# A graph-network kernel: another order of its beginning, gathers one tile ahead, and a step that gathers a whole block

## The reference, cut to what matters

```python
xs, xd = x[edge_src], x[edge_dst]                     # 53125 x 32 each
sh1 = sqrt(3) * edge_vec / norm(edge_vec)
w  = mlp(emb, fc1_w1, fc1_w2)                          # 10 -> 16 -> 512 per edge
s_t, v_t = bilinear(xs, xd, sh1, w)
w2 = mlp(emb, fc2_w1, fc2_w2)                          # 10 -> 16 -> 384 per edge
scal, gates, vecs = bilinear2(s_t, v_t, sh1, w2)
edge_out = concat(tanh(scal), vecs * tanh(gates)) * norm
return layernorm(x + segment_sum(edge_out, edge_dst))  # 3125 x 32
```

## Time and profile before

| | us |
|---|---|
| runs of the kernel before | 744.56, 744.84, 747.78 (median 744.84) |
| the profiled execution | 744.64 |
| its span, first to last instruction | 742.8 |
| PE busy / DVE busy / ACT busy / POOL busy | 687.2 / 691.7 / 560.2 / 528.0 |
| mean granted PE clock | 0.97 |
| first instruction of the first products (L751) | 37.64 |

### The profile page before, as it was taken

How to read it: one execution, slowest core, us unless ns; L and a number is a source line. 1 busy time by engine, 2 the same in 40 slices (tenths; PEclk the granted TensorE clock), 3 DMA queues, 4 the chain that set the end, 5 groups by cost and what they waited for, 6 DMA issues and landing times.

```text
span 742.8 us, 19328 instructions
## 1 busy us (share of the span) xinstructions
PE 687.2 (93%) x5990; PEld 282.9 (38%) x5990; DVE 691.7 (93%) x1231; ACT 560.2 (75%) x1281; POOL 528.0 (71%) x653
## 2 busy tenths in 40 slices
PE   2359999999999999999999999999999999999984
PEld 2113334434443444344344444334434443444321
DVE  7488999999999999999999999999999999999986
ACT  3238887887888778888888888877788888878752
POOL 5676888778876887688768886787778876887200
PEclk7569999999999999999999999999999999999998
DMA  5412211111111211121112111211121111111000
GB/s 132 112 34 47 47 32 28 40 46 28 30 42 27 50 26 42 28 47 31 43 26 45 29 43 27 48 31 27 40 46 29 28 39 26 41 27 27 20 1 23
DMA packets 45822, 28.49 MB, mean 38 GB/s; under 512 B 23299, under 2 KB 43941, under 8 KB 45721
## 3 DMA queue, kind: packets, MB, share of 16 engines
q1 hardware_dynamic: 31402, 19.43, 9.9%
q0 software_dynamic: 13312, 6.84, 6.0%
q10 hardware_dynamic: 1006, 0.96, 0.5%
HBM read 22.46 MB, written 4.74 MB: 37 GB/s over the span
## 4 chain that ended last, share of the span: by engine, by line
PE 87%; DVE 4%; issue 2%; ACT 1%; POOL 1%; DVEq 0%; ACTq 0%
PE ps L1073 16%; PE ps L986 14%; PE ps L1004 13%; PE ps L993 9%; PE ps L1053 8%; PE ps L974 6%; PE ps L1029 5%; PE ps L1066 4%; PE ps L1060 3%; PE ps L964 3%; PE ps L1041 3%; PE ps L948 2%; PE ps L1021 2%; DVE p_s L751 2%; ACT v_s L528 1%
## 5 line engine op out<-in xcount | busy, mean ns | idle before, releaser
L374 POOL DMA_INDIRECT xs<-in_xp,src_i x416 | 401.0, 964 | 115.2 <-issue 104.3
L751 DVE TENSOR_TENSOR p_s<-ps,h 128x2048 f32<-128x2048 f32 x104 | 238.3, 2292 | 21.6 <-PE ps L1073 20.9
L791 DVE TENSOR_TENSOR z_s<-ps,h 128x2048 f32<-128x2048 f32 x104 | 237.6, 2284 | 1.3 <-PE ps L1029 1.2
L528 ACT CAST v_s<-ps 128x512 bf16<-128x512 f32 x312 | 182.2, 584 | 48.3 <-PE ps L986 43.2
L1073 PE MATMUL ps<-f,w_f 32*128 32x512 f32 x832 | 119.7, 642 | 4.3
L986 PE MATMUL ps<-p_s,sum_m 128*32 128x512 f32 x832 | 111.7, 605 | 0.6 <-DVE p_s L751 0.5
L1004 PE MATMUL ps<-z_s,w_z 128*32 128x512 f32 x832 | 110.8, 605 | 1.5 <-DVE z_s L791 1.5
L494 ACT COPY f<-ps 128x512 f32<-128x512 f32 x104 | 61.0, 587 | 41.9 <-PE ps L974 41.5
L993 PE MATMUL ps<-v_s,less 128*128 128x512 bf16 x208 | 81.1, 390 | 2.8 <-ACT v_s L528 2.6
L416 POOL TENSOR_TENSOR along<-fe,r 128x192 f32<-128x192 f32 x104 | 54.2, 521 | 32.8 <-ACT fe L506 26.3
L1053 PEld LDWEIGHTS ps<-ident,u 128*128 128x128 f32 x416 | 43.8, 141 | 87.6 <-issue 87.0
(11 more groups left out here) (129 smaller groups left out, 848.7 us busy)
## 6 DMA issues: line engine op xcount, KB each, us to landing
emb<-e_dram SPq DMA_DIRECT2D x309, 30.0 KB
xs<-in_xp,src_i POOLq DMA_INDIRECT x416
e_dram<-e_part SPq DMA_DIRECT2D x7, 360.0 KB, 3.0
e_in<-in_emb SPq DMA_DIRECT2D x8, 240.0 KB, 2.9
window<-x_dram SPq DMA_DIRECT2D x104, 7.9 KB
eo_all<-in_vec_t SPq DMA_DIRECT2D x1, 528.0 KB, 5.0
x_dram<-eo_all SPq DMA_DIRECT2D x1, 525.0 KB
place<-place_dram SPq DMA_DIRECT2D x26, 20.0 KB
```

The lines of the kernel that those rows point to most:

```text
L374: nc.gpsimd.indirect_dma_start(xs_r[n][:, t, :], None, xp, bass.IndirectOffsetOnAxis(src_i[:, m * T + t:m * T + t + 1], axis=0)).then_inc( ...
L528: nc.scalar.copy(v_s[:], v_ps).then_inc(v_step, 1)
L751: nc.vector.tensor_tensor(p_s[:], ps[:, 0:4, :], h1_r[m % 2][:].unsqueeze(1).to_broadcast([128, 4, BE]), ALU.mult).then_inc(p_done, 1)
L791: nc.vector.tensor_tensor(z_s[:], ps[:, 0:4, :], h2_r[k % 3][:].unsqueeze(1).to_broadcast([128, 4, BE]), ALU.mult).then_inc(z_done, 1)
```

## The change

It touches the setup of all engines, steps up to 8 of the loop, and the places of a few operations of the super-blocks. In words:

- ACT issues the load of the first `src_i` as its first transfer, and the rest of the directions' vectors (`vt`, 528 KB) in its setup; both were SP's.
- Block 0's features come by themselves (`e_whole`, `w_whole`, four small loads of SP): `hidden_1(0)` and `hidden_2(0)` are f32 matmuls on them, and no longer wait for `e_dram`. The first super-block's parts: rests by DVE instead of POOL, the second part by ACT in step -3, the store by SP.
- The third part of x is made by DVE directly. SP stores x ahead of loading the first places, loads three window bases ahead, and stores the rest of the places behind the first three windows.
- `acc` is zeroed by ACT (four activations) in its setup instead of DVE in the loop; `dst_f` goes.
- DVE makes `spread` earlier, `rep_m`, `w_first`, `w_z` and `centre` later (steps 0, -1, 0 and 3), and spreads the eight steps of the other directions over i = -1, 1, 2, 2, 2, 3, 3, 4.
- PE reads the misfit flag in step -3 instead of ahead of `spread_places(0)`.
- POOL gathers ten tiles ahead of its branch instead of four, and then by the order below. From step 9 on its gathers stand as before.
- ACT's `copy_sources` stands at the end of its step from i = -1 to 8, behind `copy_rows` from 9 on (before: behind it from 2 on).
- Later super-blocks: POOL's first rest one step later, ACT's second part one, POOL's second rest two, the store one.

```diff
+WHOLE = 1
+DEEP = 8
-            sp.dma_start(src_i[:, 0:TA], src_t[:, 0:TA]).then_inc(src_loaded, 16)
+            for n in range(2):
+                sp.dma_start(e_whole[32 * n:32 * n + HID], emb[0:WHOLE * HID].rearrange("(b h) e -> h b e", h=HID)
+                             ).then_inc(whole_loaded, 16)
+                sp.dma_start(w_whole[32 * n:32 * n + HID], w1[0:HID, n, :]).then_inc(whole_loaded, 16)
             load_super(0)
...
-            sp.wait_ge(place_stored, 16)
-            load_places(0)
             sp.wait_ge(x_part_ready, PARTS)
...
-            sp.dma_start(of_blocks[FIRST:NB], place_part[FIRST:NB]).then_inc(place_stored, 16)
+            sp.wait_ge(place_stored, 16)
+            load_places(0)
             sp.wait_ge(bases_loaded, 16)
+            first_bases = [sp.value_load(bases[0:1, m:m + 1], min_val=0, max_val=N - 1) for m in range(3)]
             sp.wait_ge(x_stored, 48)
             load_window(0)
             load_window(1)
-            sp.wait_ge(emb_zeroed, 1)
             load_window(2)
-            load_emb(1)
-            sp.dma_start(vt[:, TA:TILES, :], vec_t[:, TA:TILES, :]).then_inc(vect_rest_loaded, 16)
+            sp.dma_start(of_blocks[FIRST:NB], place_part[FIRST:NB]).then_inc(place_stored, 16)
+            sp.dma_start(w_z[:].rearrange("p n c -> p (n c)"), w2b).then_inc(w2b_loaded, 16)
             load_window(3)
+            store_super(0)
...
+            sp.wait_ge(emb_zeroed, 1)
+            load_emb(1)
+            load_emb(2)
...
             pool.wait_ge(src_loaded, 16)
-            gather(0, 0, 3)
-            rest_of_emb(0, 0)
-            gather(0, 3, T)
+            gather(0, 0, T)
+            gather(1, 0, T)
+            gather(2, 0, 2)
             pool.wait_ge(misfits_ready, 1)
...
+                    if 0 <= i <= DEEP:
+                        gather(i + 4, 1, T)
+                    elif real(i + 5) and i > DEEP:
+                        gather(i + 5, 0, 3)
+                    if real(i + 3):
+                        directions(i + 3)
+                    if i == -2:
+                        gather(2, 2, T)
+                        gather(3, 0, 2)
+                    if i == -1:
+                        gather(3, 2, T)
+                    later_emb(i)
+                    if -1 <= i < DEEP:
+                        gather(i + 5, 0, 1)
+                    elif i == DEEP:
+                        gather(i + 5, 0, T)
+                    elif real(i + 5) and i > DEEP:
+                        gather(i + 5, 3, T)
...
+            act.dma_start(src_i[:, 0:TA], src_t[:, 0:TA]).then_inc(src_loaded, 16)
             act.dma_start(dst_row_i, dst_rows).then_inc(dst_rows_loaded, 16)
...
             part_of_x(1)
+            act.dma_start(vt[:, TA:TILES, :], vec_t[:, TA:TILES, :]).then_inc(vect_rest_loaded, 16)
             part_of_emb(0, 0)
-            part_of_x(2)
-            part_of_emb(0, 1)
+            clean = acc[:].rearrange("p (n c) -> p n c", c=128)
+            for first, end in ((0, 7), (7, 13), (13, 19), (19, 25)):
+                nc.scalar.activation(clean[:, first:end, :], ident[:].unsqueeze(1).to_broadcast([128, end - first, 128]), ACT.Copy,
+                                     scale=0.0).then_inc(acc_zeroed, 1)
...
-            act.wait_ge(e_part_ready, PARTS)
-            act.dma_start(e_dram[:, 0:SB * HID, :].rearrange("n r e -> r n e"), e_part[0:SB * HID]).then_inc(e_stored, 16)
             copy_oht(0)
-            act.wait_ge(emb_zeroed, 1)
-            act.wait_ge(e_stored, 16)
-            for first in (0, 32, 64):
-                act.dma_start(emb_r[0][first:first + PARTS * HID], e_dram[:, 0:HID, :]).then_inc(emb_loaded[0], 16)
             for i in STEPS:
...
-                if i == -1:
+                if i == 2:
                     act.wait_ge(n2_ready, 2)
                     nc.scalar.activation(nrm_t[:, TA:TILES], n2_t[:, TA:TILES], ACT.Sqrt).then_inc(norm_ready, 1)
...
+                if i == 0:
+                    repeat_constants()
                 if real(i + 2):
                     sum_along(i + 2)
+                if i == -1:
+                    first_weights()
+                    directions(0, TA, TILES).then_inc(r4_step, 1)
                 if i == 0:
+                    second_weights()
+                if i == 3:
                     late_constants()
 
-                for step, at_step in enumerate((-2, -2, 0, 0, 0, 1, 1, 1)):
+                for step, at_step in ((1, 1), (2, 2), (3, 2), (4, 2), (5, 3), (6, 3), (7, 4)):
```

More of the change, by code:

```diff
@@ L149, in program @@
         w2a_s = early(128, 2 * 128).rearrange("p (n c) -> p n c", n=2)
+        e_whole = early(32 + HID, WHOLE * BE).rearrange("p (b e) -> p b e", b=WHOLE)
+        w_whole = early(32 + HID, 128)
         xd = sb("xd", [128, T, D])
@@ L444, in _ @@
                     if i == -3:
-                        gather(2, 0, T)
+                        gather(2, 2, T)
                     if real(i + 4) and i + 4 >= 3:
@@ L618, in _ @@
                     copy_f(i + 2)
+                if real(i + 3) and -1 <= i <= DEEP:
+                    copy_sources(i + 3)
                 later_emb(i)
@@ L707, in _ @@
             nc.vector.tensor_copy(spread[:], spread_s[:]).then_inc(spread_ready, 1)
+            dve.wait_ge(dst_rows_loaded, 32)
+            link(nc.vector.tensor_copy(base_f[:], base_i[:]))
+            link(nc.vector.tensor_copy(place_f, dst_row_i))
+            link(nc.vector.tensor_scalar(place_f, place_f, base_f[:], None, ALU.subtract))
+            nc.vector.engine_nop().then_inc(place_ready, 1)
+            nc.vector.tensor_tensor(place_sq, place_f, place_f, ALU.mult).then_inc(place_ready, 1)
+            rest_of_x(0)
+            dve.wait_ge(place_step, 3)
+            nc.vector.tensor_tensor(place_part[:, 2, :], place_sq, place_part[:, 1, :], ALU.subtract).then_inc(place_step, 1)
+            rest_of_x(1)
+            link(nc.vector.tensor_scalar(bad, place_f, float(WIN), None, ALU.is_ge))
+            link(nc.vector.scalar_tensor_tensor(out=bad, in0=place_f, scalar=0.0, in1=bad, op0=ALU.is_lt, op1=ALU.add))
+            nc.vector.tensor_reduce(ext[0:NB], bad, AX.X, ALU.add).then_inc(misfit_parts, 1)
+            link(directions(0, 0, TA))
+            directions(1, 0, TA).then_inc(n2_ready, 1)
+            rest_of_emb(0)
+            dve.wait_ge(misfit_sum, 1)
+            nc.vector.tensor_copy(misfits[:], ps[0:1, 7, 0:1]).then_inc(misfits_ready, 1)
             for step in range(2, 7):
@@ L731, in _ @@
             nc.vector.tensor_scalar(less[0][:], ident[:], of_part[:, 1:2], -1.0, ALU.mult, ALU.mult).then_inc(rep_step, 1)
-            for g in range(4):
-                link(nc.vector.tensor_scalar(sel_g[:, g, :], sel_w[:], of_group[:, g:g + 1], of_part[:, 0:1], ALU.mult, ALU.mult))
-                nc.vector.tensor_copy(rep_m[:, g], sel_g[:, g, :].unsqueeze(1).to_broadcast([128, 16, 8])).then_inc(rep_step, 1)
-            def late_constants():
-                dve.wait_ge(weights_loaded, 48)
+            rest_of_emb(1)
@@ new lines, in _, with repeat_constants @@
+            c1, c2 = 0.25 / math.sqrt(32.0), 1.0 / 16.0
+            dve.wait_ge(w2a_loaded, 16)
+            link(nc.vector.tensor_scalar(w_f[:], w2a_s[:, 1, :], c1 * SQRT3, None, ALU.mult))
+            nc.vector.scalar_tensor_tensor(out=w_f[:], in0=w2a_s[:, 0, :], scalar=c1, in1=w_f[:], op0=ALU.mult,
+                                           op1=ALU.add).then_inc(weights_ready, 1)
+            def repeat_constants():
+                for g in range(4):
+                    link(nc.vector.tensor_scalar(sel_g[:, g, :], sel_w[:], of_group[:, g:g + 1], of_part[:, 0:1], ALU.mult, ALU.mult))
+                    nc.vector.tensor_copy(rep_m[:, g], sel_g[:, g, :].unsqueeze(1).to_broadcast([128, 16, 8])).then_inc(rep_step, 1)
@@ new lines, in first_weights @@
+            def first_weights():
+                dve.wait_ge(w1_loaded, 16)
+                link(nc.vector.tensor_copy(w_first[:], w1_s))
+                link(nc.vector.tensor_tensor(w1_s, w1_s, w_first[:], ALU.subtract))
+                link(nc.vector.tensor_copy(w1_mid, w1_s))
+                nc.vector.tensor_copy(w_first[32:64], w1_mid[32:64]).then_inc(weights_ready, 1)
+                nc.vector.tensor_tensor(w_first[64:96], w1_s[64:96], w1_mid[64:96], ALU.subtract).then_inc(weights_ready, 1)
@@ L744, in late_constants @@
-                nc.vector.memset(acc[:], 0.0).then_inc(acc_zeroed, 1)
+            def late_constants():
+                link(nc.vector.tensor_copy(iota[:], iota_i[:]))
                 link(nc.vector.tensor_reduce(strip_sum[:], ident[:].rearrange("p (g c) -> p c g", g=4), AX.X, ALU.add))
@@ L1056, in hidden_1 @@
             def hidden_1(m):
-                pe.wait_ge(emb_loaded[m % 3], 48 * (m // 3 + 1))
+                if m < WHOLE:
+                    pe.wait_ge(whole_loaded, 64)
+                    nc.tensor.matmul(h1_ps, w_whole[0:HID], e_whole[0:HID, m, :], start=True, stop=True).then_inc(h1_done, 1)
```

(12 more changed lines are left out.)

138 lines of the change are left out of this document (55 added, 83 removed).

## The result

The changed kernel takes **735.64 us** (731.73 to 737.30, 4 executions) against 745.34 for the kernel before (4 executions): ratio 0.985, 95% interval 0.982 to 0.988. That is 9.7 us less, where 8.5 were forecast from the medians then shown. Six more executions of the same kernel, taken later, gave 736.52, ratio 0.988 (0.985 to 0.991). The profiled execution happens to be the fastest of its four, 731.73 with a span of 729.9; I come back to this.

The account below looks back on a forecast made before the run. PE was taken as the bound from 90.3 us on, DVE close behind, with time lost in the beginning. Earlier steps were to bring the eighth products 8.3 us forward: 744.64 - 8.3 = 736.3 us, range 731 to 742.

Parts of the forecast that it names:

- p(7): Start of the eighth products: 82.0 us instead of 90.31, 8.3 us earlier, moving the end by as much.
- Ahead of the loop: Setup: x stores at 11.3 us, windows at about 15.8, ACT's first one-hot copied at about 16 instead of 19.79.
- POOL up to d(0): POOL's setup: free at 4.5 us, ten gathers of 14.2, branch 3.32; first directions at 22.0 instead of 26.81.
- rival A: More is hidden: first directions at 19.0 us, eighth products at 77.8 to 80, total 732 to 734; chance 0.17.
- rival B: POOL is later: ten gathers at 1.7 us each, first directions at 24.8 to 27.1, total 739.1 to 741.4; chance 0.14.
- p(0): Start of the first products: 28.5 us instead of 37.64, set by DVE and PE alike.
- p(1): Start of the second products: 34.7 us instead of 49.41, by PE's 6.2 us from the first products.
- p(2) to p(3): Third to fourth products, 42.6 to 53.4 us: DVE waits 1.2 for ACT's square root, then a 4.05 stretch.
- the one I costed at nothing: POOL's new order up to step 8: 5.89 us a block against PE's 6.507, cover 7 us, no cost.
- C: Given back: DVE's stall in step 2 and its extras keep PE's clock low, 742.4 us, no measurable difference; chance 0.12.
- D: Slower: POOL bounds steps 0 to 9 if 49 gathers take 1.64 us each instead of 1.25; chance 0.06.
- E: Step 8's whole block and the later `copy_sources` are hidden, all gain comes from the beginning; within the forecast, no separate chance.

Follow-up runs that it names:

- again: Second profile of the changed kernel, no edit, execution of 734.55 us; that set of six executions measured 736.52 us, ratio 0.988 to the kernel before.
- after: First profile of the changed kernel, the fastest of its first four executions, 731.73 us; their median was 735.64 us.
- one operation a step: Changed kernel with DVE's seven operations on the later directions one per step in steps 1 to 7, instead of three in step 2: 734.69 us, ratio 0.986.
- the spread gathers: Changed kernel with step 8's three extra POOL gathers taken one each in steps 8, 11 and 14: 732.02 us, ratio 0.982 to the kernel before.
- the fillers: Changed kernel with 23 more idle PE matmuls in its setup: 734.84 us, ratio 0.987; with the spread gathers 731.20, and with more idle matmuls 733.24.

## Why the prediction was right, and where its steps were not

**The forecast held, by its mechanism.** The eighth products were to come 8.3 us earlier; they came 11.0 (again) and 13.9 us (after). The last came 10.1 and 12.9 earlier, and the median fell by 9.7. Shown by taking each part back: block 0 by itself 4.4 us, `acc` off DVE 3.4, ten tiles ahead 4.3 by the ratios, each known to within some 2.7 us. They add to 12.1, more than the 8.9 of the same kernel's ratio, but the excess isn't clear of noise. If it is real, it would fit their standing in one chain, so that with one of them gone the others' work waits; no run tests that. SP's new order and the places of DVE's steps on the later directions, beyond one operation a step, were not taken back by themselves.

**The number is nearer than its steps, and that is partly luck.** Against the forecast p(7) was 2.7 us ahead (again), 1.4 of which p(11) gave back. And I took the ending as fixed ("the last steps are not touched"), where one and the same ending takes 27.7 to 31.2 us by the clock.

**Ahead of the loop** right in size: x stores at 11.28 (11.3 forecast), windows at 16.47 (15.8), ACT's first one-hot at 16.96 (16).

**POOL up to d(0)**: its queue was sized well, wrongly ended. The list landed at 5.0 (4.5) and ten gathers ended at 18.30 (18.7). But I added the 3.32 of the branch behind them, and that time is not POOL's own work: it runs from an event in the setup, and more gathers only cover it. With four gathers ahead POOL came out of it at 18.46; with ten it had read the flag at 14.4, ended its gathers at 18.30, and waited for ACT's copy until 19.73. So d(0) was 19.7 to 20.4, near rival A's 19.0, and waited for ACT, where I had said that it would not. This term was 1.6 to 2.3 us too late. Nine of the ten gathers took 0.94 to 1.20 us, one 1.61 (in the second profile eight, and two of 1.60 and 1.67), while DVE was busy 13.6 of the 15 us from 5 to 20. Ten took 13.3 us, 1.33 each with their issue, not 1.7, and rival B fell with it. The Trainium skill's rule behind that rival (GPSIMD Engine Reference, Key points), that GpSimd shares its SBUF interfaces with VectorE and contends with its instructions that have two SBUF inputs, shows in one or two gathers of the ten at most.

**p(0)** 25.7 to 26.6 for 28.5: the earlier d(0), carried on. **p(1)** 31.3 or 35.3 for 34.7: I took one duration, 6.2 us from p(0), from rows in which the clock was 0.85 in the mean; there are two, 5.65 with the clock back at 25 us and 8.66 at 0.50 throughout. **p(2) to p(3)**: 9.6 us in both profiles for 10.8. The stretch of reciprocal and two multiplies took 3.39 (4.05), the wait for ACT's square root 0.88 (1.2). As forecast, PE stood idle for it and was slow behind it, in the first profile:

```profile
44.82 2.35 DVE L677 RECIPROCAL eo_all<-eo_all 128x352 f32<-128x352 f32 x1 [0.88 <-ACT eo_all L603]
...
50.56 0.39 PE L1063 MATMUL ps<-v_s,rep_m 32*128 32x512 bf16 x4 [3.09 <-DVE p_s L776]
53.60 2.09 PE L1117 MATMUL ps<-f,w_f 32*128 32x512 f32 x8
```

PE waits 3.09 us for the products, and the first layer behind takes 2.09 instead of 1.14. The windows behind p(3) in the first profile, then in the second:

```profile
50.00:60.00 10.00, 9.42 (x63) 3.08 (x64) 9.79 (x18) 6.51 (x14) 3.33 (x5) 0.83 0.10 17
50.00:60.00 10.00, 6.53 (x54) 2.73 (x52) 9.79 (x17) 5.66 (x12) 5.27 (x7) 1.00 0.12 24
```

In the second the clock did not fall, and still p(3) to p(7) took 28.0 us there and 28.2 in the first, 28.6 by the forecast: with DVE busy 9.79 of the 10 us in both, the low clock behind p(3) cost 0.2 us at most.

**The step that failed** is the one I costed at nothing: "from d(3) on it gains on PE", with a cover of 7 us for the whole block of step 8. I had POOL run from d(3) at its own 5.89 us a block. But each `directions(m)` also waits for ACT's copy of the sources, which the change puts at the end of ACT's step, so POOL can never be ahead of ACT. The page's group of the operation over all blocks, then the row of POOL's timeline at d(6):

```profile
L428 POOL TENSOR_TENSOR along<-fe,r 128x192 f32<-128x192 f32 x104 | 53.9, 518 | 51.9 <-ACT fe L510 48.6
```

```profile
59.99 0.51 POOL L428 TENSOR_TENSOR along<-fe,r 128x192 f32<-128x192 f32 x1 [5.75 <-ACT fe L510]
```

When DVE and PE stall behind p(3), ACT stalls with them, and POOL stands 5.75 us ahead of d(6) and loses there what it had gained. From d(3) = 36.12, which was 3.7 earlier than forecast, my working (eight blocks at 5.89, 2.4 of rests, 9.9 for the whole block) gives d(12) = 95.5; it came at 102.53, and 6.4 of the 7.0 between are such waits (0.47, 5.75 and 0.18). In the second profile they are 8.5. Without the lump p(11) would have come 6.49 behind p(10), at 102.41, for which d(12) had to start by 101.1. So the cover was 5.6 us, and the seven gathers overran it by 1.4. I asked what the head of POOL's queue waits for at d(2), and should have asked it at each step up to 8.

**The rivals.** A came half true: d(0) early, and p(7) at 76.4 to 79.3 (77.8 to 80). C showed for one block, in one of the two profiles. D: behind p(3) DVE waited for POOL once, 1.53 us for d(12) of POOL's step 9, and that cost 1.4 us; it was one of my signs of being wrong. E is true in the main, that all comes from the beginning, but not in its word "hidden": the feature that the change is named for wins 0.6 us at p(3) and costs 1.4 us where the lead is made.

**Left open.** What sets when PE's clock comes back and whether it falls at the end; and, with it, 3 of the 4.5 us by which the spread gathers beat the changed kernel's median. Four kernels with them have medians of 731.2 to 733.2 and ratios 0.981 to 0.983; the version to keep is the one with spread gathers, the fillers adding nothing that can be told.

## What to carry to other kernels

Count the beginning back to one event per block, and for each queue ask what its head waits for: an engine that waits once a block for its neighbour can't bank its idle time, so work taken ahead in one lump goes on the path while the same work in three pieces is hidden. A latency that follows an event (a branch on a flag) is not added to the work before it; it is the later of the two that counts. A large instruction moved off the bounding engine brings its own length and the idle time just ahead of it (3.3 us for 2.73 in step 3). Where it brings more, look first for what else in the stretch became shorter: here it was two multiplies, not the clock of the engine that idled behind. And compare intervals between two events that lie close together, not their distance from the start, when executions of one kernel part early.

## What the runs showed of the hardware that was not expected

PE's granted clock after the setup is not a property of the kernel. The same instructions had it back at 25 us in one execution and at 35 in another, which cost 2.2 us. What PE did ahead of it doesn't settle it either. The changed kernel's first profile, then the kernel with one operation a step, whose instructions are the same up to there:

```profile
16.00:24.00 8.00, 5.71 (x43) 3.81 (x47) 5.46 (x22) 5.02 (x14) 5.18 (x8) 0.50 0.52 126
```

```profile
16.00:24.00 8.00, 5.70 (x43) 3.81 (x47) 5.35 (x21) 5.01 (x14) 5.17 (x8) 0.50 0.50 126
24.00:32.00 8.00, 8.00 (x32) 2.45 (x33) 6.76 (x14) 2.96 (x7) 6.10 (x8) 0.50 0.34 89
```

PE is equally busy in both, and in the second the clock comes back only at about 33 us. With fillers it fell at 20 while PE was busy nearly all the time. In the last 30 us it may fall too, for up to 3.5 us more (27.7 to 31.2 from the last products on). Together these are as large as the 5.6 us between the fastest and slowest execution of the changed kernel, and more than most edits here are worth; that they are the whole of it is not shown, since the slowest executions have no trace. The mean clocks say the same: in the changed kernel's second set 0.981 went with 733.8 and 0.969 with 737.7. The Trainium skill (TensorE: Matmul & The Clock Gate, Part 1) says that the way to the full clock varies from run to run and costs under 1% of a typical kernel's span. The traces agree: it varied, and the difference was 2.2 us, 0.3% of the span. That is still almost a quarter of this change's gain.
